# A decoder layer on one core: FFN weight scales spread by a DRAM round trip instead of matmuls with diagonals, and w_q loaded behind the seventh expert

## The chip, the core and the metric

The kernel runs on one core of one Trainium2 chip. The metric is device time in microseconds (us) from start to end of one execution; lower is better. The engines are named as in the profile: PE (TensorE, matmuls; PEld is its weight load), DVE (VectorE), ACT (ScalarE), POOL (GpSimd) and SP (SyncE, which here issues DMAs only).

## The reference, cut to what matters

One decoder layer in three parts, each added to the residual and followed by a layer norm: a Mamba block with a mixture of experts, a cross-attention, and a feed-forward with 8-bit weights and activations.

```python
# x: (4, 256, 256); 1024 tokens of 256.  Every token goes to 2 of 8 experts.
x = layernorm(x + moe(mamba(x)))
# cross-attention: 16 heads of 128, 64 keys for each batch entry
q = rmsnorm((x @ Wq).reshape(B, Sq, H, D), gq)
k = rmsnorm((ctx @ Wk).reshape(B, Skv, H, D), gk)
x = layernorm(x + (softmax(q k^T / sqrt(D)) (ctx @ Wv)) @ Wo)
# feed-forward, every linear with fp8 weights and one scale for each output row
def qlinear(qx, scale_x, scale, W, idx, out_idx=None):
    Wr = W[:, idx]
    w_scale = max(abs(Wr), axis=1, keepdims=True) / 448
    qw = fp8(Wr / w_scale)
    y = (qx * scale_x) @ (qw * w_scale).T * scale
    return y if out_idx is None else y[:, out_idx]
t = silu(qlinear(qx, sx, sc, w_gate, up_idx, down_idx)) * qlinear(qx, sx, sc, w_up, up_idx, down_idx)
x = layernorm(x + qlinear(quantised t, ..., w_down, down_idx))
```

The change concerns `w_scale`: 704 scales of `w_gate`, 704 of `w_up`, 256 of `w_down`. They are worked out with one weight row on each partition, so that a chunk of 128 scales is a column (`w_scale[:, m, chunk]`, m = 0, 1, 2). They are used as factors along the free dimension of token tiles, so each partition needs all of them in a row (`scale_rows[m]`).

## The kernel before

All tensors that live for a part of the kernel are views of one buffer, `arena`, by address in KB; the names `arena` and `ps` (the eight PSUM banks) are therefore all that the profile shows of most operands. Every engine has a program written out by hand, in the order in which it runs; engines wait for each other on counting semaphores (`pe.wait_ge(s["x_normed"], 4)`). No scheduler moves anything.

The part of the program that matters runs from the experts to the start of the attention:

- **Experts.** For each of the 8 experts PE runs a tail of 64 rows and then a loop of full tiles of 128 rows (matmuls L2177 up, L2185 down). POOL gathers the rows of each tile from DRAM (L466) and scatters the results to `moe_out` in DRAM (L499). The weights of expert e are loaded by SP (L303) into `w_moe[e % 2]`, two buffers at 163 KB (even experts) and at 16.5 KB (odd ones), when the expert two before is done. Beside the experts DVE quantises the FFN weights in pieces (`quantise`, L1275; its tables are `QUANT_AHEAD` and `QUANT_BEHIND`), and in that leaves `w_scale`. `gate_tail` (L1439) is DVE's part of an expert's tail, for which PE waits (L2122).
- **After the experts.** PE transposes the last keys (L2101) and multiplies keys by `w_qT` (L2200: 16 pairs of matmuls; ACT takes each from PSUM, L891). Meanwhile SP waits until all results are stored, loads them back in four parts (`y_got`, L347) and then loads `w_q` (L348, 2 MB, into 16.5 KB). DVE adds the parts to `x` (`add_results`, L1510), takes the variances and normalises the first four tiles (L1508), which raises `x_normed` to 4; then it does the same for the other four.
- **Scales.** DVE multiplies `w_scale[:, 1]` by `down_one` (L1493) and makes three sets of diagonal matrices from the columns (L1494, helper L1069). PE multiplies them by a matrix of ones (`spread_scales`, helper L1927), in three places: before the transposes of `x` (L2214), behind them (L2323) and behind the first scores (L2327). ACT copies each result to `scale_rows` (`take_scales`, L895). The buffer of `scale_rows` is the one that the experts' rows come into, hence PE's wait for the last gather (L2203).
- **Attention and FFN.** PE then runs the list at L2322 ff.: transposes of `x` (`transpose_x1`, L2220; DVE copies one bank, L1525, ACT the other, L903), scores of a token tile (L2239), queries (L2250), transposed probabilities (L2262), values (L2271), and between them the FFN of earlier tiles (L2286 gate and up). DVE's `take_gate` (L1595) and `take_up` (L1599) read `scale_rows[0]` and `[1]`, `add_result` (L1631) `scale_rows[2]`.

## Time and profile before

| | |
|---|---|
| three timed runs, us | 634.47, 634.90, 635.46 (median 634.9) |
| profiled execution, first to last instruction, us | 633.6 |
| PE busy | 586.3 us (93%) |
| DVE busy | 468.6 us (74%) |
| ACT busy | 386.8 us (61%) |
| POOL busy | 299.3 us (47%) |
| chain that ended last | PE 70%, ACT 12%, DVE 9%, issue 5%, DMA 2% |
| mean granted TensorE clock | 0.988 of full speed |

The times are of whole executions, the profile is of one more execution; its span leaves out what lies before the first and behind the last instruction, and the median is 1.3 us above it. The busy shares are means over a program of very different stages: the scan of the Mamba block (to about 245 us) is set by DVE and ACT, the experts (to about 442 us) by PE with short waits for DVE, the attention with the FFN by PE up to about 576 us, and the last 57 us by chains that go back and forth between DVE, PE and ACT. The chain of waits follows the end of the program back, from each instruction to the one that released it.

### The profile page before, as it was taken

To read this page: it belongs to the slowest core of one execution; us is meant where nothing else is said; L and a number is where in the kernel's file an instruction comes from. 1 tells how busy PE (TensorE), PEld (TensorE's weight loads), DVE (VectorE), ACT (ScalarE), POOL (GpSimd) and SP (SyncE) were. 2 spreads that over 40 slices of the span, in tenths; PEclk is the share of its full clock that TensorE was granted. 3 is DMA by queue.
4 is the path that set the end of the run, shared out by engine and by line. 5 is a ranking of instruction groups with operands and counts; after the bars stand their busy time and mean duration, and the time that the engine had idled before them with its cause. 6 is when DMAs were issued, how large, how long until landed. Compare 5 with 4: busy or idle time off the path is not lost.

```text
span 633.6 us, 10935 instructions
## 1 busy us (share of the span) xinstructions
PE 586.3 (93%) x3641; PEld 443.9 (70%) x3641; DVE 468.6 (74%) x793; ACT 386.8 (61%) x880; POOL 299.3 (47%) x239
## 2 busy tenths in 40 slices
PE   4999689998999999999999999999999999998874
PEld 2653579887998888597779779778855555665542
DVE  6989999999999976534553543563655789998885
ACT  4689899999999956522232231321746665687543
POOL 6032599999999991123232334344112232225101
PEclk9999899999999999999999999999999999999898
DMA  8001552121121008334441441411700000000002
GB/s 286 2 1 38 168 221 61 51 61 57 51 64 55 34 17 322 109 141 171 171 150 55 171 170 34 171 43 28 274 1 1 1 2 0 1 1 1 2 0 67
DMA packets 18261, 51.50 MB, mean 81 GB/s; under 512 B 3842, under 2 KB 9603, under 8 KB 16548
## 3 DMA queue, kind: packets, MB, share of 16 engines
q1 hardware_dynamic: 15172, 41.43, 19.0%
q0 software_dynamic: 2752, 7.34, 4.0%
q10 hardware_dynamic: 288, 2.10, 0.9%
q8 instruction: 27, 0.44, 0.3%
q14 instruction: 22, 0.18, 0.1%
HBM read 46.21 MB, written 4.66 MB: 80 GB/s over the span
## 4 chain that ended last, share of the span: by engine, by line
PE 70%; ACT 12%; DVE 9%; issue 5%; DMA 2%; POOL 0%; POOLq 0%; DVEq 0%; ACTq 0%
PE ps L2177 11%; PE ps L2250 8%; ACT arena L672 7%; PE ps L2185 6%; PE ps L2239 4%; PE ps L2271 4%; ACT arena L687 3%; PE ps L1960 3%; PE ps L1945 3%; PE ps L1994 2%; PE ps L2200 2%; PE ps L1786 2%; PE ps L2117 2%; PE ps L1795 2%; PE ps L1947 2%
## 5 line engine op out<-in xcount | busy, mean ns | idle before, releaser
L449 POOL TENSOR_TENSOR arena<-arena 128x1024 f32<-128x1024 f32 x63 | 147.3, 2391 | 3.4 <-DVE arena L1305 3.1
L1305 DVE TENSOR_TENSOR_SCAN arena<-arena,ps 128x1024 f32<-128x1024 f32 x64 | 143.4, 2279 | 4.0 <-ACT arena L672 0.9
L672 ACT ACTIVATE arena<-arena,a_neg 128x510 f32<-128x510 f32 x128 | 84.6, 709 | 1.9 <-DVE arena L1305 1.7
L2177 PEld LDWEIGHTS ps<-arena 128*128 128x128 f32 x660 | 75.4, 192 | 3.4 <-issue 3.1
L2177 PE MATMUL ps<-arena 128*128 128x128 f32 x660 | 77.0, 276 | 0.0
L1945 PE MATMUL ps<-ident,arena 128*128 128x128 f32 x384 | 64.7, 278 | 9.9 <-ACT arena L683 8.5
L1960 PE MATMUL ps<-ident,arena 128*128 128x128 f32 x512 | 67.3, 273 | 2.5 <-DVE arena L1314 1.8
L882 ACT ACTIVATE arena<-ps 128x256 f32<-128x256 f32 x45 | 17.3, 384 | 82.5 <-PE ps L2177 82.5
L687 ACT ACTIVATE arena<-arena,b_tok 128x512 f32<-128x512 f32 x96 | 64.8, 709 | 0.0
L1960 PEld LDWEIGHTS ps<-ident,arena 128*128 128x128 f32 x512 | 57.8, 141 | 4.1 <-DVE arena L1314 1.3
L2250 PE MATMUL ps<-arena 128*128 128x512 f32 x128 | 58.2, 595 | 0.0
L1945 PEld LDWEIGHTS ps<-ident,arena 128*128 128x128 f32 x384 | 45.7, 143 | 14.6 <-ACT arena L683 12.8
L1947 PE MATMUL ps<-arena 128*128 128x128 f32 x256 | 49.9, 277 | 0.0
L528 POOL TENSOR_TENSOR q_rs<-q_ms,neg_half 128x16 f32<-128x16 f32 x8 | 23.6, 2948 | 51.5 <-DVE q_ms L1555 51.5
L914 ACT ACTIVATE arena<-ps 128x128 f32<-128x128 f32 x128 | 33.5, 279 | 17.9 <-PE ps L2250 17.8
L2185 PE MATMUL ps<-arena 128*128 128x256 f32 x180 | 41.3, 379 | 0.0
L1482 DVE TENSOR_TENSOR arena<-arena,ps 128x256 f32<-128x256 f32 x30 | 12.6, 421 | 37.9 <-ACT arena L882 37.4
L499 POOL DMA_INDIRECT moe_out<-arena,result_now x23 | 23.8, 1035 | 34.8 <-DVE arena L1490 21.4
L2250 PEld LDWEIGHTS ps<-arena 128*128 128x128 f32 x128 | 23.5, 190 | 23.7 <-issue 20.8
L1947 PEld LDWEIGHTS ps<-arena 128*128 128x128 f32 x256 | 39.1, 193 | 0.0
L2185 PEld LDWEIGHTS ps<-arena 128*128 128x128 f32 x180 | 33.0, 190 | 3.9
L466 POOL DMA_INDIRECT arena<-hn_rows,row_now x23 | 25.4, 1105 | 18.2 <-POOL row_now L484 18.2
(313 smaller groups left out, 1143.6 us busy)
## 6 DMA issues: line engine op xcount, KB each, us to landing
arena<-in_w_moe SPq DMA_DIRECT2D x8, 2176.0 KB, 9.0
arena<-c_dram SPq DMA_DIRECT2D x32, 256.0 KB, 3.2
arena<-in_w_o ACTq DMA_DIRECT2D x1, 2048.0 KB, 13.1
arena<-in_w_qT SPq DMA_DIRECT2D x1, 2048.0 KB, 11.5
arena<-moe_out SPq DMA_DIRECT2D x8, 256.0 KB, 4.7
arena<-in_w_q SPq DMA_DIRECT2D x1, 2048.0 KB, 10.2
x<-in_x SPq DMA_DIRECT2D x2, 512.0 KB, 4.5
arena<-in_w_in SPq DMA_DIRECT2D x2, 512.0 KB, 5.6
```

What stands on the lines that cost most here:

```text
L449: pool.tensor_tensor(in_chunks(hC[unit % 3]), in_chunks(h[unit % 3]), c_bc[:, m % C_BUFS, :].unsqueeze(1).to_broadcast([P, 2, HALF]), ALU. ...
L466: pool.indirect_dma_start(row_in, None, hn_rows[:, :], bass.IndirectOffsetOnAxis(index, 0)).then_inc(s["ld_rows"], 16)
L672: ins = nc.scalar.activation(dA_b[:, unit % 2, 2 * k:2 * k + 2, 1:], dt_b[:, c, 2 * half:2 * half + 2, 1:], ACT.Exp, scale=a_neg[:, c, n:n ...
L687: nc.scalar.activation(sdtx[m % 2][:, i, :], dtxT[:, HALF_TILES * half + i, :], ACT.Identity, scale=b_tok[:, HALF_TILES * half + i, n:n + ...
L914: ins = nc.scalar.activation(q_junk[:, g % 2, hd * DH:(hd + 1) * DH], ps[:, g % 2, hd * DH:(hd + 1) * DH], ACT.Square, scale=float(DH) ** ...
L1305: nc.vector.tensor_tensor_scan(h[unit % 3], dA[:, k, :], ps[:, 2 * k:2 * k + 2, :].rearrange("p a b -> p (a b)"), 0.0, ALU.mult, ALU.add). ...
L1945: ins = nc.tensor.transpose(dst, sdtx[m % 2][:, i, c * P:(c + 1) * P], ident[:, :])
L1947: ins = nc.tensor.matmul(dst, dtxT[:, HALF_TILES * half + i, c * P:(c + 1) * P], b_diag[m % 2], start=True, stop=True)
L1960: return nc.tensor.matmul(ps[:, bank, c * P:(c + 1) * P], part, ident[:, :], start=first, stop=last, is_transpose=ADD_TRANSPOSED, skip_gro ...
L2177: ins = nc.tensor.matmul(ps[:, bank, c * P:(c + 1) * P], w13[:, k, chunk * P:(chunk + 1) * P], xT[:, k, :], start=(k == 0), stop=(k == KD ...
L2185: ins = nc.tensor.matmul(ps[:, 6, 0:D], hid[:, c, :], w2[:, c, :], start=(c == 0), stop=(c == FCH - 1))
L2250: ins = nc.tensor.matmul(ps[:, g % 2, :], tokens(t, k), w_q[:, k, g * HALF:(g + 1) * HALF], start=(k == 0), stop=(k == KD - 1))
```

## The change

The scales no longer pass through DVE, PE and ACT. DVE multiplies `w_scale[:, 1]` by `down_one` in the turn of expert 3 and signals it. SP, once it has issued the weights of expert 5, writes all 14 columns of `w_scale` to DRAM in the transposed order (1792 single values of 4 bytes), and later reads them back into every partition in one broadcast (`all_scales`, 7 KB for each partition, at the old address of `scale_rows`). It does so when PE has finished the ninth of the 16 pairs at L2200; PE's wait for the last row gather moves from behind these pairs to before the ninth. DVE waits for the read before the first `take_gate`. DVE's diagonals, PE's spread matmuls and ACT's copies are gone, with the waits around them.

`w_q` gets the even experts' buffer (163 KB) and is loaded when expert 6, the last to use it, is done; PE waits for it on `ld_o`. `y_got`, `shift` and `soft`, which were there, move to the odd experts' buffer (16.5 KB).

```diff
+SCALES = 2 * FCH + KD
-        y_got = [view(163, [TILES, D]), view(171, [TILES, D])]
+        y_got = [view(16.5, [TILES, D]), view(24.5, [TILES, D])]
-        w_qT, w_q = view(0, [HEADS, D]), view(16.5, [KD, HEADS * DH])
+        w_qT, w_q = view(0, [HEADS, D]), view(163, [KD, HEADS * DH])
-        shift, soft, pT = view(163, [2, HEADS, KV]), view(171, [2, HEADS, KV]), view(0, [2, PAIRS, P])
+        shift, soft, pT = view(16.5, [2, HEADS, KV]), view(24.5, [2, HEADS, KV]), view(0, [2, PAIRS, P])
-        diag = [view(87.5, [FCH, P]), view(66.5, [FCH, P]), view(69.5, [KD, P])]
+        all_scales = view(56.5, [SCALES * P])
+        scale_dram = nc.dram_tensor("scale_dram", (1, SCALES * P), F32).ap()
+        SCALES_READY_AT, SCALES_STORED_AT, ROWS_LANDED_AT = 3, 4, 8
...
                 load_weights(e + 1)
+                if e == SCALES_STORED_AT:
+                    sp.wait_ge(s["scales_ready"], 1)
+                    sp.dma_start(scale_dram.rearrange("o (k p) -> p (o k)", p=P), w_scale[:, :, :].rearrange("p m c -> p (m c)")[:, 0:SCALES],
+                                 allow_slow_non_contiguous=True).then_inc(s["ld_idx"], 16)
+            done = sp.value_load(bounds[0:1, E - 1:E], min_val=1, max_val=OUT_TILES)
+            sp.wait_ge(s["y_ready"], done + 1)
+            load(w_q, inp["w_q"], "ld_o")
             total = sp.value_load(bounds[0:1, E:E + 1], min_val=E, max_val=OUT_TILES)
             sp.wait_ge(s["y_stored"], total * 16)
...
-            load(w_q, inp["w_q"], "ld_kq")
+            sp.wait_ge(s["kv_psum"], QK_AT + ROWS_LANDED_AT + 1)
+            sp.wait_ge(s["ld_idx"], 96)
+            load(all_scales, scale_dram.partition_broadcast(P), "ld_idx")
...
-            take_scales(0)
             take_result_half(0)
-            take_scales(1)
-            take_scales(2)
             mean_squares(0, 0, 1, 2, 3)
...
+                if e == SCALES_READY_AT:
+                    nc.vector.tensor_tensor(w_scale[:, 1, :], w_scale[:, 1, :], down_one[:, :], ALU.mult).then_inc(s["scales_ready"], 1)
                 gate_tail(e, last)
...
-            link(nc.vector.tensor_tensor(w_scale[:, 1, :], w_scale[:, 1, :], down_one[:, :], ALU.mult))
-            for m, chunks in enumerate((FCH, FCH, KD)):
-                diagonals(diag[m], w_scale[:, m, 0:chunks], chunks).then_inc(s["counted"], 1)
...
                 dve.wait_ge(s["ff_psum"], 2 * t + 1)
+                if t == 0:
+                    dve.wait_ge(s["ld_idx"], 112)
...
                 bank = kv_bank()
+                if n == ROWS_LANDED_AT:
+                    pe.wait_ge(s["ld_rows"], last * 16 + 32)
...
-            pe.wait_ge(s["ld_rows"], last * 16 + 32)
...
-            spread_scales(0)
...
             transpose_x1(0)
-            spread_scales(1)
             pe.wait_ge(s["kv_out"], kv[0])
             pe.wait_ge(s["x1T_done"], 2)
             scores_of(0)
-            spread_scales(2)
-            pe.wait_ge(s["ld_kq"], 48)
+            pe.wait_ge(s["ld_o"], 32)
             queries_of(0, 0, 1, 2, 3)
-            pe.wait_ge(s["spread_done"], 5)
             transpose_x1(1)
```

How the instructions stand on PE behind the last pair at L2200, before (a program's list of each engine's instructions with the semaphores that they wait for; L1927 are the spread matmuls, L2220 the transposes of `x`, L2239 the first scores, L2250 the first queries):

```order
L1927 MATMUL ps<-arena,ones 128x512 [waits kv_out,counted,ld_rows]
L1927 MATMUL ps<-arena,ones 128x256
L2220 MATMUL ps<-ident,x 128x128 [waits x_normed]
L2220 MATMUL ps<-ident,x 128x128 x7
L1927 MATMUL ps<-arena,ones 128x512 [waits kv_out,counted]
L1927 MATMUL ps<-arena,ones 128x256
L2239 MATMUL ps<-arena 128x512 [waits x1T_done,kv_out]
L2239 MATMUL ps<-arena 128x512 x3
L1927 MATMUL ps<-arena,ones 128x256 [waits spread_done,counted]
L2250 MATMUL ps<-arena 128x512 [waits ld_kq]
L2250 MATMUL ps<-arena 128x512 x3
```

The five spread matmuls stand in three places among transposes, scores and queries. On the same engine and at the same place in the changed program (where L2201 are the transposes, L2220 the scores and L2231 the queries):

```order
L2201 MATMUL ps<-ident,x 128x128 [waits x_normed]
L2201 MATMUL ps<-ident,x 128x128 x7
L2220 MATMUL ps<-arena 128x512 [waits x1T_done,kv_out]
L2220 MATMUL ps<-arena 128x512 x3
L2231 MATMUL ps<-arena 128x512 [waits ld_o]
L2231 MATMUL ps<-arena 128x512 x3
```

The five are gone; transposes, scores and queries follow each other in the same order. SP's list in the changed program from the weights of expert 5 on (L306 are expert weights, L347 the write of the scales, L280 all other loads; the ISA and REGISTER rows fetch the tile counts that its waits use):

```order
L306 DMA arena<-in_w_moe 128x4352 [waits y_ready]
L347 DMA scale_dram<-w_scale 128x14x1 [waits scales_ready]
...
L306 DMA arena<-in_w_moe 128x4352 [waits y_ready]
...
L280 DMA arena<-in_w_q 128x4096 [waits y_ready]
L352 TENSOR_LOAD bounds
L352 ISA x2
L353 REGISTER_ALU
L280 DMA arena<-moe_out 128x2x256 [waits y_stored]
L280 DMA arena<-moe_out 128x2x256 x7
L280 DMA arena<-scale_dram 128x1792 [waits ld_idx,kv_psum]
```

Before, nothing stood between the expert weights and the loads of `moe_out`, and `w_q` was behind these as SP's last load; now `w_q` is before them, the write of the scales is between the weights of experts 5 and 6, and their read is the last load.

## Rows read from the trace of the kernel before

**Rows 1.** Chain of waits, 442 to 504 us: start us, length us, what.
```profile
444.64 13.81 PE ps L2200 x64
458.46 1.29 PE ps L1927 x4
...
460.62 1.29 PE ps L1927 x4
461.91 3.43 PE ps L2239 x8
465.35 0.43 PE ps L1927 x2
...
502.93 1.19 PE ps L2286 x8
```
**Rows 2.** Timeline of DVE, 443 to 474 us: start, length, instruction, [idle before it, releaser].
```profile
443.60 2.16 DVE L1069 TENSOR_TENSOR arena<-ident,w_scale 128x768 f32<-128x768 f32 x3
449.62 1.67 DVE L1518 SCALAR_TENSOR_TENSOR x<-arena,prob,x 128x256 f32<-128x256 f32 x4 [3.86 <-DMA arena<-moe_out]
...
452.37 1.67 DVE L1518 SCALAR_TENSOR_TENSOR x<-arena,prob,x 128x256 f32<-128x256 f32 x4 [0.41 <-DMA arena<-moe_out]
...
457.48 1.36 DVE L1508 TENSOR_SCALAR x<-x,mv,rs 128x256 f32<-128x256 f32 x4
...
473.86 0.17 DVE L1555 TENSOR_SCALAR q_ms<-q_ms 128x16 f32<-128x16 f32 x1 [5.20 <-ACT arena L914]
```
**Rows 3.** Timeline of PE and ACT around the first scores.
```profile
459.58 1.04 PE L2220 MATMUL ps<-ident,x 128*128 128x128 f32 x8
...
460.66 0.60 ACT L903 ACTIVATE arena<-ps 128x512 f32<-128x512 f32 x1
...
461.75 3.60 PE L2239 MATMUL ps<-arena 128*128 128x512 f32 x8
...
465.62 7.03 PE L2250 MATMUL ps<-arena 128*128 128x512 f32 x16
```
**Rows 4.** DMA issues: what, by which queue, count, KB each, median us to landing.
```profile
arena<-in_w_q SPq DMA_DIRECT2D x1, 2048.0 KB, 10.2
```
**Rows 5.** DMA queues, whole program: packets, MB, share of 16 engines' span.
```profile
q1 hardware_dynamic: 15172, 41.43, 19.0%
```
**Rows 6.** DMA queues, 18 to 22 us, where L300 reads single values.
```profile
q1 hardware_dynamic: 1009, 0.00, 12.8%
```
**Rows 7.** Timeline of DVE and PE at the tail of expert 3.
```profile
328.09 0.19 DVE L1284 RECIPROCAL w_inv<-w_scale 128x6 f32<-128x6 f32 x1
...
328.66 0.11 DVE L1442 MEMSET arena<- 64x64 f32 x1 [0.38 <-PE ps L2117]
...
329.41 0.22 DVE L1446 TENSOR_TENSOR arena<-arena,ps 64x64 f32<-64x64 f32 x1
...
329.69 0.55 PE L2125 MATMUL ps<-ident,arena 128*128 128x128 f32 x3
```
**Rows 8.** Row gathers (L466): all, and in the chain of waits the longest.
```profile
DMA to landing us min/median/max: 2.7/3.1/7.0
...
268.45 6.96 DMA arena<-hn_rows,row_now
```
**Rows 9.** Timelines: DVE in expert 5, POOL in expert 7; chain in expert 7.
```profile
381.40 0.42 DVE L1452 COPY arena<-ps 64x256 f32<-64x256 f32 x1 [3.21 <-POOLq L491]
...
424.33 0.99 POOL L466 DMA_INDIRECT arena<-hn_rows,row_now  x1 [0.79 <-POOL row_now L484]
...
431.37 0.22 PE ps L2087 x2
```
**Rows 10.** Windows near the end: us, busy (x) of PE, PEld, DVE, ACT, POOL; clock; DMA.
```profile
582.00:588.00 6.00, 3.24 (x18) 2.50 (x18) 5.86 (x10) 3.17 (x13) 2.91 (x1) 0.72 0.02 4
588.00:594.00 6.00, 6.00 (x28) 4.56 (x27) 4.71 (x6) 4.46 (x6) 1.68 (x1) 0.71 0.00 1
...
612.00:618.00 6.00, 2.96 (x18) 1.16 (x16) 5.62 (x10) 2.65 (x5) 0.00 (x0) 1.00 0.00 0
```

More of the change, by code:

```diff
@@ L231, in build @@
             s_shifted s_exp s_soft pT_psum pT_done attn_psum attn_taken eps4 rstd_x2 ld_idx ld_late gathered_w0
-            gathered_w1 iota_done counted spread_psum spread_done quantised wT_psum wT_done x_scaled x_size_ready x_quant
+            gathered_w1 iota_done scales_ready spread_psum spread_done quantised wT_psum wT_done x_scaled x_size_ready x_quant
             xT8_psum xT8_done ff_psum ff_read ff_gate ff_in t_scaled t_in_ready t_size_ready prod_done t_done t_psum
@@ L893, in _ @@
                 step += 1
-            def take_scales(m):
-                act.wait_ge(s["spread_psum"], 3 + m)
-                bank = (4, 6, 4)[m]
-                width = (FCH, FCH, KD)[m] * P
-                nc.scalar.activation(scale_rows[m], ps[:, bank:bank + 2, :].rearrange("p a b -> p (a b)")[:, 0:width], ACT.Identity).then_inc(s["spread_done"], 1)
             def take_result_half(half):
@@ L1066, in _ @@
             dve.wait_ge(s["iota_done"], 1)
-            def diagonals(dst, col, chunks):
-                return nc.vector.tensor_tensor(dst, ident[:, :].unsqueeze(1).to_broadcast([P, chunks, P]),
-                                               col.unsqueeze(2).to_broadcast([P, chunks, P]), ALU.mult)
             def compare_up():
@@ L1637, in _ @@
             add_epsilon(0)
-            dve.wait_ge(s["spread_done"], 5)
             take_result_half(1)
@@ L1922, in _ @@
             transpose_inputs(1, 1)
-            def spread_diagonals(diagonals, chunks, bank):
-                for at in range(0, chunks, 4):
-                    n = min(4, chunks - at)
-                    ins = nc.tensor.matmul(ps[:, bank + at // 4, 0:n * P], ones[:, :], diagonals[:, at:at + n, :].rearrange("p a b -> p (a b)"), start=True, stop=True)
-                ins.then_inc(s["spread_psum"], 1)
-            SPREAD_BANKS = (4, 6, 4)
             def inputs_of(unit):
@@ L2202, in _ @@
                 ins.then_inc(s["kv_psum"], 1)
-            pe.wait_ge(s["ld_rows"], last * 16 + 32)
-            def spread_scales(m):
-                pe.wait_ge(s["counted"], 1 + m)
-                if m == 2:
-                    pe.wait_ge(s["spread_done"], 3)
-                else:
-                    pe.wait_ge(s["kv_out"], kv[0] - 4 + 2 * m)
-                spread_diagonals(diag[m], (FCH, FCH, KD)[m], SPREAD_BANKS[m])
-            spread_scales(0)
             def transpose_x1(half):
```

## Prediction, written before the changed kernel ran

> **What bounds the kernel now.** I read the chain of waits first, since the busy shares are means over stages with different limits. From 442 to 576 us it is PE almost without a break, and the three places where the change takes work away stand in it as pieces of their own: 1.29, 1.29 and 0.43 us of L1927 among the pairs of L2200, the scores and the queries [rows 1]. So PE sets the time where the spread matmuls stand, and what they take, 3.01 us in sum, is the most that their removal by itself can return. The chain does not say what is late next. For that I read the timelines of DVE, ACT and PE just there. The first four tiles of `x` are normalised at 457.48 + 1.36 = 458.84 us [rows 2], while PE ends L2200 at 458.46 [rows 1]. PE was never seen waiting for DVE because the first spread filled the gap; without it, DVE is 0.4 us late.
>
> **The change part by part.**
>
> *Before the transposes.* DVE's L1508 ends at 458.84 [rows 2]. PE starts about 0.06 us after the DVE instruction that it waits for: L1446 ends at 329.63, L2125 starts at 329.69 [rows 7]. So the transposes start at 458.90; before, it was 459.58 [rows 3], a gain of 0.68.
>
> *Between transposes and scores.* The scores need both copied banks. The eight transposes take 1.04 us, to 459.94. ACT's L903 started 0.04 us after their end (459.58 + 1.04 = 460.62; it started at 460.66) and took 0.60 [rows 3]. So the copy ends at 459.94 + 0.04 + 0.60 = 460.58, and the scores start 0.06 later, at 460.64. Before, it was 461.75 [rows 3], since the second spread stood there; it covered the copy, so its 1.29 us bring only another 0.43. The gain so far is 1.11. ACT is free for L903: the copies of the scales that stood around it are gone.
>
> *Between scores and queries.* Scores to queries took 465.62 - 461.75 = 3.87 us [rows 3], 0.43 of it the third spread [rows 1]. Without it the queries start at 460.64 + 3.44 = 464.08, which is 1.54 us sooner. That is the sum: 3.01 us of PE work go, 1.54 arrive, and the rest becomes two gaps on PE, some 0.4 us for `x_normed` and some 0.7 us for the copy.
>
> *From there to the end.* Every later instruction of PE, ACT, DVE and POOL hangs on the queries and scores, or on work that was early. DVE comes to the first scores only some 0.7 us sooner (its own chain of adds is unchanged), but it then waited 5.20 us for the queries' squares [rows 2], so it takes up the whole 1.54. The lists are otherwise the same, so I carry the 1.54 to the end undiminished.
>
> *DVE's diagonals.* They took 2.16 us from 443.60, and then DVE sat idle for 3.86 us until the first part of the results had come from DRAM [rows 2]. Their removal lengthens that wait: nothing.
>
> *DVE's multiplication in expert 3.* It is one instruction on 128x6 like the reciprocal before it, 0.19 us [rows 7]. It stands between this reciprocal, which ends at 328.28, and `gate_tail`, whose L1442 sat idle for 0.38 us waiting for PE [rows 7]. PE's wait is the cover: nothing. Without the cover it would be 0.19, since PE starts L2125 right behind L1446.
>
> *The write of the scales.* 1792 values of 4 bytes, from SP, beside expert 4's gathers. The trace has no such write. The nearest row is L300's reads of single values: 1009 packets took 12.8% of 16 engines in 4 us, 8.2 us of engine time, 8.1 ns each [rows 6]. At that price 1792 take 14.5 us of engine time, 0.9 us on 16 engines. The upper end is the mean packet of the queue, which carries 2.7 KB: 19.0% of 16 x 633.6 us over 15172 packets is 127 ns [rows 5], 14.2 us on 16 engines. I take 0.9, the row with the same size of packet. What hides it: SP has nothing to issue until the next weights, and the row gathers that share the engines usually land in 3.1 us [rows 8], while PE comes for a row some 7 us after its gather (424.33 to 431.37, in a loop that is the same for all full tiles) [rows 9]. The longest gather took 7.0 us [rows 8], so even that would be in time, barely. Cost nothing; at the upper end perhaps 0.5 us for one late gather.
>
> The Trainium skill's page "DMA: Bandwidth & Descriptors" (Rules for kernel authors) says that a strided last dimension becomes one descriptor for each element, and its Specifications that transfers under 512 B are read, modified and written back. The trace agrees with the first (1009 packets for some 960 values); no row shows the second. If it doubles the price, the write takes an estimated 1.8 us, which the same slack hides.
>
> *w_q in expert 7.* It took 10.2 us to land [rows 4] and did not hold PE: the queries followed the scores. Now it is loaded some 40 us sooner, so it cannot hold them either. It runs beside expert 7's gathers, as expert weights do in experts 2 to 6. There DVE waits up to 3.21 us for a result to be stored (L1452) [rows 9], but PE's chain shows no wait for it. I take nothing. The upper end is a late gather: one of 7.0 us, issued at 424.33, would land at 431.33, just before PE's 431.37. A gather of 8.5 us would cost 1.5.
>
> *The read of the scales.* It is issued after nine of 16 pairs, at about 444.64 + 9 x 0.86 = 452.4 [rows 1], behind the result loads in its queue. 0.9 MB should need less than `w_q`'s 10.2 us for 2 MB [rows 4], so it lands by 463; the first gate matmuls start at 502.93 [rows 1]: 40 us of cover. DVE's new wait is never felt. PE's earlier wait for the last gather comes some 7 us after that gather was due: nothing.
>
> **The rivals.**
>
> (a) *The result loads land sooner.* DVE waited 0.41 us for the second part [rows 2], with `w_q` queued right behind these loads. If `w_q` slowed them, its move brings up to 0.41 more: 1.95 in all, 632.95. Against: the loads of one queue start in order. PE's end of L2200 forbids more.
>
> (b) *Less arrives.* If the copies or the DVE adds start later than worked out, for instance behind the read of the scales, only the third spread and a little more are gained, about 0.5: 634.4.
>
> (c) *A stalled gather.* `w_q` or the write of the scales holds one gather for 8.5 us instead of at most 7.0 [rows 8]; PE stands 1.5 us and the gain is used up: 634.9. Speaking for it: the longest gather, 6.96 us, was in the chain [rows 8].
>
> (d) *Slower: the clock falls in the new gaps.* PE now idles some 1.1 us between 458.4 and 460.7 where it had no idle time. In 582 to 594 us, with PE busy 3.24 us of the first six, the granted clock was 0.72 and 0.71 (stretches at 1.2 instead of 2.4 GHz) [rows 10]. That is 0.28 x 6 + 0.29 x 6 = 3.4 us of PE work lost. The same fall here, where PE is the bound, ends at 634.9 - 1.5 + 3.4 = 636.8; it decides from a loss of 1.5. Against: in 612 to 618 PE was busy only 2.96 us of six and the clock stayed at 1.00 [rows 10], and my gaps are short.
>
> (e) *The late fall goes.* Everything behind 464 us shifts; if the fall at 582 does not come, another 3.4 go: 630.0. Against: the gap on PE before it is made by DVE and stays, and three runs lie within 1.0 us.
>
> **How the numbers follow.** The profiled execution spans 633.6 us, which becomes 632.1; the median of the timed runs is 634.9, 1.3 above the span, and I take the 1.54 from it: 633.4. Chances: this forecast 0.58, (a) 0.13, (b) 0.12, (c) 0.06, (d) 0.06, (e) 0.05. The range 632.2 to 635.2 holds the forecast, (a), (b) and (c) with the runs' scatter of half a us, and leaves (d) and (e) out. About 0.2% (1.3 us) is what a measurement of this kernel can tell from no change; that is 633.6, close to my forecast, so I count 0.40 of its 0.58 as faster and 0.18 as the same. Faster: 0.40 + (a) 0.12 + (e) 0.05 = 0.57. Same: 0.18 + (a) 0.01 + (b) 0.12 + (c) 0.04 = 0.35. Slower: (d) 0.06 + (c) 0.02 = 0.08.
>
> **What would show it.** In the chain of the changed kernel L1927 is absent, and between the pairs and the transposes a short piece of DVE (L1508's successor) or "issue" stands, then one of ACT before the scores. The pairs end when they did, the transposes start at about 458.9 and the queries at about 464.1. SP shows `w_q` issued near 420 and the scales' read near 452.5, with no DVE wait for it before the gate. I am wrong if PE waits for a gather in expert 4 or 7, if the clock is under 1.00 between 458 and 475, or if the last 60 us differ in length by more than 0.5 us.

## The result: slower by 0.75%, lost in expert 4

The changed kernel takes 640.16 us (median of six runs, 638.73 to 642.60), the kernel before 635.18 (six runs, 634.47 to 637.43). The ratio is 1.0075, with a 95% interval of 1.0057 to 1.0093. The profiled executions span 638.4 and 633.6 us.

To see where the 4.8 us lie, I cut both spans at four instructions that both kernels have: POOL's stores of the last tile of experts 3, 4, 6 and 7. First the kernel before, timeline of POOL (start us, length us, instruction, idle before it and its releaser):

```profile
350.35 0.99 POOL L499 DMA_INDIRECT moe_out<-arena,result_now  x1 [1.44 <-DVE arena L1490]
...
373.94 1.19 POOL L499 DMA_INDIRECT moe_out<-arena,result_now  x1 [1.44 <-DVE arena L1490]
...
420.59 1.20 POOL L499 DMA_INDIRECT moe_out<-arena,result_now  x1 [1.33 <-DVE arena L1490]
...
443.18 1.20 POOL L499 DMA_INDIRECT moe_out<-arena,result_now  x1 [1.45 <-DVE arena L1490]
```

The same four in the changed kernel, where the line is L511, with the gather (L478) behind the first of them:

```profile
351.29 0.99 POOL L511 DMA_INDIRECT moe_out<-arena,result_now  x1 [1.44 <-DVE arena L1491]
355.02 1.00 POOL L478 DMA_INDIRECT arena<-hn_rows,row_now  x1 [0.79 <-POOL row_now L496]
...
381.49 1.18 POOL L511 DMA_INDIRECT moe_out<-arena,result_now  x1 [1.44 <-DVE arena L1491]
...
428.13 1.20 POOL L511 DMA_INDIRECT moe_out<-arena,result_now  x1 [1.25 <-DVE arena L1491]
...
451.12 1.20 POOL L511 DMA_INDIRECT moe_out<-arena,result_now  x1 [1.45 <-DVE arena L1491]
```

With the start of the queries (465.78 before, 472.50 after, in the chains of waits) the span falls into six stages:

| stage | before, us | after, us | difference |
|---|---|---|---|
| start to the last store of expert 3 | 350.35 | 351.29 | +0.94 |
| expert 4 | 23.59 | 30.20 | **+6.61** |
| experts 5 and 6 | 46.65 | 46.64 | 0.0 |
| expert 7 | 22.59 | 22.99 | +0.40 |
| last store to the queries | 22.60 | 21.38 | -1.22 |
| queries to the end | 167.82 | 165.90 | -1.92 |

Expert 4 is where the scales are written. The first stage has nothing of the change but DVE's short multiplication; over all the kernels below it ends between 349.7 and 352.2 us, so its +0.94 is scatter.

**Expert 4.** The chain of waits of the changed kernel (start, length, what) shows a store of results that took 12.06 us to land. In DVE's list the copy of the tail's result (L1451) waits for that store to free its buffer, and the hidden product of the next tile (L1483) stands behind it; PE waits for the product.

```profile
351.29 12.06 DMA moe_out<-arena,result_now
...
363.41 0.43 DVE arena L1451
...
364.79 0.43 DVE arena L1483
...
365.26 2.93 PE ps L2168 x12
...
437.70 1.60 PE ps L2168 x12
```

PE's timeline shows the standstill, 3.42 us:

```profile
365.26 2.93 PE L2168 MATMUL ps<-arena 128*128 128x128 f32 x12 [3.42 <-DVE arena L1483]
...
368.41 4.07 PE L2176 MATMUL ps<-arena 128*128 128x256 f32 x12
```

Then PE ran slowly: the last two rows of the chain are the same twelve matmuls in experts 4 and 7, 2.93 and 1.60 us. The twelve of L2176 behind them took 4.07 us, where the next tile's take 2.76. Standstill and slow matmuls make some 6.1 of the 6.6 us. The windows (us, busy time of PE, PEld, DVE, ACT and POOL, granted clock, DMA share, GB/s) show the clock at 0.50, its lower level of 1.2 GHz, behind the standstill, and next to no DMA packet that begins between 360 and 364 us (the DMA share counts a packet where it begins):

```profile
358.00:360.00 2.00, 2.00 (x19) 2.00 (x18) 0.07 (x1) 0.45 (x1) 0.00 (x0) 1.00 1.07 85
360.00:362.00 2.00, 1.84 (x17) 1.65 (x15) 0.00 (x0) 0.50 (x2) 0.00 (x0) 1.00 0.00 0
362.00:364.00 2.00, 0.00 (x0) 0.00 (x0) 0.55 (x2) 0.26 (x1) 0.18 (x1) 1.00 0.04 2
...
366.00:368.00 2.00, 2.00 (x12) 2.00 (x11) 0.00 (x0) 0.00 (x0) 1.72 (x2) 0.50 0.14 33
```

POOL's queue (q0 of the DMA queues: packets, MB, share of 16 engines) moved the following from 351 to 360 us:

```profile
q0 software_dynamic: 96, 0.26, 15.8%
```

That is 0.26 MB, one store and one gather of a tile of 0.13 MB each; from 360 to 362 us the queue moved a single packet of no size that shows. The packed trace has it packet by packet: 61 of the 64 packets of 4 KB that carry the two had ended by 360.04 us, and the last three, which took 1.33 to 4.28 us each, ended at 362.68, 364.01 and 364.13. Yet the store landed at 363.35, and the gather, issued at 355.02, is the one that took 11.0 us (rows 8 showed at most 7.0 [rows 8]):

```profile
DMA to landing us min/median/max: 2.7/3.1/11.0
```

The write of the scales had been queued from 350.87 us, behind the weights of expert 5, and all but a dozen of its packets had gone by 360.05.

A DMA raises its semaphore in 16 steps and has landed with the last; the packed trace has the time of each step. Of the store's steps 15 came between 357.91 and 359.19 us and the last at 363.34. The write's came between 363.76 and 366.14, and the gather's between 363.96 and 366.03. Taken in order, 15 of the gather's 16 follow one of the write's by 0.14 to 0.21 us. So the gather, most of whose data had moved by 360, was told as landed step by step with the write.

**Behind the experts** the profile reads as forecast in kind. Chain of waits, changed kernel, to be held against [rows 1]:

```profile
451.12 2.89 DMA moe_out<-arena,result_now
...
455.47 4.93 DMA arena<-moe_out
460.43 1.67 DVE x L1516 x4
...
465.62 1.29 DVE x L1506 x4
466.95 1.11 PE ps L2201 x8
468.08 0.61 ACT arena L909
468.83 3.67 PE ps L2220 x8
472.50 6.87 PE ps L2231 x16
```

The spread matmuls are gone, and the end of the pairs of matmuls no longer sets the transposes: it is now the landing of the results, through DVE's adds (L1516) and normalisation (L1506). PE's timeline has the two new gaps, 0.56 us for `x` and 0.78 for ACT's copy:

```profile
466.95 1.09 PE L2201 MATMUL ps<-ident,x 128*128 128x128 f32 x8 [0.56 <-DVE x L1506]
468.83 3.67 PE L2220 MATMUL ps<-arena 128*128 128x512 f32 x8 [0.78 <-ACT arena L909]
```

**The end.** The two windows in which the clock was 0.72 and 0.71 before [rows 10] are now:

```profile
582.00:588.00 6.00, 6.00 (x23) 3.07 (x21) 4.73 (x14) 4.37 (x18) 2.11 (x2) 1.00 0.00 0
588.00:594.00 6.00, 3.09 (x22) 1.85 (x20) 5.79 (x12) 4.17 (x18) 2.91 (x1) 1.00 0.00 1
```

The last stage has two lengths in the fourteen profiled kernels of this study, 165.8 to 165.9 us in eight and 167.1 to 167.8 in six. It is long in the two that keep the spread matmuls (the kernel before and the write alone) and in four of the other twelve. That alone cannot rule out a link to the change. But the kernel with the write behind the loads, one of the eight, has a mean granted clock of 0.988 over its twelve timed runs, the same as the kernel before over the 27 beside them.

### The profile page after: what moved, and what is told of

Same layout as the page of the kernel before. It is cut to its first block, busy times and chain, and to the rows that moved or that the text cites. A ratio compares the mean times of both kernels' runs of the same rounds, so it can differ in the third digit from the quotient of the medians.

```text
span 638.4 us, 10912 instructions
## 1 busy us (share of the span) xinstructions
PE 585.3 (92%) x3631; PEld 443.4 (69%) x3631; DVE 465.5 (73%) x790; ACT 384.6 (60%) x877; POOL 299.4 (47%) x239
## 4 chain that ended last, share of the span: by engine, by line
PE 61%; ACT 13%; DVE 11%; DMA 8%; issue 5%; POOL 1%; SPq 0%; DVEq 0%; POOLq 0%; ACTq 0%
PE ps L2168 10%; PE ps L2231 8%; ACT arena L684 7%; PE ps L2176 6%; DMA moe_out<-arena,result_now 5%; PE ps L2220 4%; ACT arena L699 3%; PE ps L2252 3%; PE ps L1951 3%; PE ps L1936 3%; PE ps L1985 2%; PE ps L1785 2%; PE ps L1794 2%; PE ps L1938 2%; DVE arena L1304 2%
## 5 line engine op out<-in xcount | busy, mean ns | idle before, releaser
L2168 PE MATMUL ps<-arena 128*128 128x128 f32 x660 | 79.1, 280 | 3.8 <-DVE arena L1483 3.7
L2168 PEld LDWEIGHTS ps<-arena 128*128 128x128 f32 x660 | 76.9, 195 | 7.8 <-DVE arena L1483 4.4
L2231 PE MATMUL ps<-arena 128*128 128x512 f32 x128 | 58.2, 595 | 0.0
L1938 PE MATMUL ps<-arena 128*128 128x128 f32 x256 | 50.3, 279 | 0.0
L2176 PE MATMUL ps<-arena 128*128 128x256 f32 x180 | 42.7, 389 | 0.0
L2231 PEld LDWEIGHTS ps<-arena 128*128 128x128 f32 x128 | 23.6, 191 | 24.1 <-issue 21.2
L511 POOL DMA_INDIRECT moe_out<-arena,result_now x23 | 23.8, 1034 | 34.5 <-DVE arena L1491 22.2
L1938 PEld LDWEIGHTS ps<-arena 128*128 128x128 f32 x256 | 39.4, 195 | 0.0
L2176 PEld LDWEIGHTS ps<-arena 128*128 128x128 f32 x180 | 34.1, 197 | 4.2
L1483 DVE TENSOR_TENSOR arena<-arena,ps 128x256 f32<-128x256 f32 x30 | 12.6, 421 | 33.4 <-ACT arena L894 31.4
L478 POOL DMA_INDIRECT arena<-hn_rows,row_now x23 | 25.4, 1104 | 18.2 <-POOL row_now L496 18.2
```

Source lines behind the costliest of these rows:

```text
L1938: ins = nc.tensor.matmul(dst, dtxT[:, HALF_TILES * half + i, c * P:(c + 1) * P], b_diag[m % 2], start=True, stop=True)
L2168: ins = nc.tensor.matmul(ps[:, bank, c * P:(c + 1) * P], w13[:, k, chunk * P:(chunk + 1) * P], xT[:, k, :], start=(k == 0), stop=(k == KD ...
L2176: ins = nc.tensor.matmul(ps[:, 6, 0:D], hid[:, c, :], w2[:, c, :], start=(c == 0), stop=(c == FCH - 1))
L2231: ins = nc.tensor.matmul(ps[:, g % 2, :], tokens(t, k), w_q[:, k, g * HALF:(g + 1) * HALF], start=(k == 0), stop=(k == KD - 1))
```

## The experiments

My theory was that the 1792 single values are the whole loss: while they are under way, row transfers of the experts land late. The rivals were `w_q` in expert 7, a place that merely happened to be bad, and the new code behind the experts. Each kernel is the changed one with the edit shown, unless said otherwise. The stage table behind the experiments holds the stages of all profiled runs.

**The write alone, on the kernel before.** DVE's multiplication moves to expert 3 and SP writes the scales in expert 4; the matmuls with diagonals stay.

```
+                if e == SCALES_STORED_AT:
+                    sp.wait_ge(s["counted"], 1)
+                    sp.dma_start(scale_dram.rearrange("o (k p) -> p (o k)", p=P), w_scale..., allow_slow_non_contiguous=True)
```

> The kernel before with one thing added: DVE multiplies w_scale[:, 1] in the turn of expert 3, and SP writes the 1792 scales to DRAM behind the weights of expert 5, as in the changed kernel; nothing reads them, and diagonals, spread matmuls and w_q stay as they were. Theory 1 (the write holds up the store of expert 3's last result tile; DVE waits in order for the one result row buffer, PE for DVE, and the clock falls in that gap): the store lands in about 12 us instead of 7.6, PE stands about 3.4 us in expert 4, the clock is at half for some 7 us behind it, and the time is about 6.5 us over before (3 to 7, as late falls of the clock come and go). Theory 2 (w_q beside expert 7 costs the time): no change against before.

Measured: 641.62 us against 635.93, ratio 1.0091 (1.0061 to 1.0121). Here not the store but the gather was held, and PE waited for it directly:

```profile
354.49 12.02 DMA arena<-hn_rows,row_now
...
366.55 0.44 PE ps L2095 x2
366.99 4.24 PE ps L2193 x12
```

Expert 4 takes 29.52 us, 5.9 more than before. The clock fell here too: twelve matmuls of 2.59 us (their length in the tile before) took 4.24. The write by itself costs as much as the whole change lost: 5.7 us here, 5.0 there.

**The write later in the same loop**, once the tail of expert 4 has been stored:

```
+                if e == SCALES_STORED_AT + 1:
+                    before = sp.value_load(bounds[0:1, e - 1:e], min_val=1, max_val=OUT_TILES)
+                    sp.wait_ge(s["scales_ready"], 1)
+                    sp.wait_ge(s["y_stored"], before * 16 + 16)
+                    sp.dma_start(scale_dram..., w_scale..., allow_slow_non_contiguous=True)
```

> The changed kernel with the write of the scales moved by some 12 us: SP waits until the tail of expert 4 has been stored and then writes, in the stretch in which no weights move, 10 us before the weights of expert 6. Theory 1: the store of expert 3's last tile lands in about 7.6 us as before, PE does not stand in expert 4 and the clock stays at 1.00 there; of the changed kernel's 6.6 us lost in expert 4 nearly all come back, so it is 5 to 7 us faster than the changed kernel and 0.5 to 2 us faster than before (the 1.2 us gained behind the experts less 0.4 us lost in expert 7). Theory 2: it stays at the changed kernel's time, about 5 us over before. If the write is bad for any store that it meets, the next store (full tile, 4 us later) lands late and some of it stays.

Measured: 642.27 us, ratio 1.0117 (1.0087 to 1.0147): a miss. The write, issued at 361.71 and no longer behind the weights, held the next gather instead:

```profile
363.24 10.58 DMA arena<-hn_rows,row_now
```

So the place was not a particularly bad one: at both places the write met a row transfer. But the hold looked different. The write's 1808 packets had gone by 363.8 us, and then the rows themselves moved slowly. In POOL's queue, from 362 to 374 us:

```profile
q0 software_dynamic: 96, 0.26, 24.3%
```

That is 46.7 us of packet time for this gather and the store behind it. Single packets of 4 KB took up to 4.03 us, where in the kernel before none at the like place took over 0.37. The write's steps came up to 372.50 us, the gather's up to 373.82.

**`w_q` behind the result loads**, the write unchanged:

```
-            done = sp.value_load(bounds[0:1, E - 1:E], min_val=1, max_val=OUT_TILES)
-            sp.wait_ge(s["y_ready"], done + 1)
-            load(w_q, inp["w_q"], "ld_o")
...
+            load(w_q, inp["w_q"], "ld_o")
             sp.wait_ge(s["kv_psum"], QK_AT + ROWS_LANDED_AT + 1)
```

> The changed kernel with w_q loaded behind the result loads again (still into 163 KB); the write of the scales stays where the change put it. Theory 1: expert 4 still loses 6 to 7 us; only the 0.4 us in expert 7 come back, perhaps less if the result loads get slower with w_q behind them; the time stays 4 to 6 us over before. Theory 2: it returns to before or below it.

Measured: 639.07 us, ratio 1.0055 (1.0032 to 1.0078). Expert 7 is back at 22.59 us; expert 4 still takes 27.37. Its store took 10.70 us and its gather 11.56:

```profile
354.55 11.56 DMA arena<-hn_rows,row_now
```

PE stood twice, for 2.05 and 1.12 us, and in this execution the clock stayed at 1.00 there. That splits the 6.6 us of the changed kernel: PE's standstill is 3.2 to 4.4 us in each of these runs, and where it came in one piece (3.42 us in the changed kernel, 3.90 with the write alone, 4.36 with the write later) slow matmuls follow; in two pieces they did not.

**The write in natural order**, one run of 56 bytes for each partition. The transposition is left out, so the scales come back in another order:

```
-sp.dma_start(scale_dram.rearrange("o (k p) -> p (o k)", p=P), ...
+sp.dma_start(scale_dram.rearrange("o (p k) -> p (o k)", p=P), ...
```

> The changed kernel with the scales written to DRAM in the order in which they lie: 128 runs of 56 bytes instead of 1792 single values, at the same place in the program and with as many bytes. The transposition is left out, so the scales that come back are in the wrong order; all times are those of the same work. Theory 1 in the form that the many single values are the cost (their packets fill the DMA engines and their completion holds back the store's): the store of expert 3's last tile lands in about 7.6 to 8.5 us, PE hardly stands in expert 4, and the time is 5 to 7 us under the changed kernel. A rival form, that any write to DRAM behind the weights holds the store: the store still lands in 11 to 12 us and the time stays.

Measured: 634.18 us against 635.93, ratio 0.9968 (0.9951 to 0.9985). No gather took over 6.0 us, no store over 8.5, and expert 4 takes 23.71. The same bytes at the same place hold nothing, so it is the way in which the single values are written. In expert 7 the chain still holds a store, with DVE's L1451 and PE behind it, which the kernels without `w_q` there do not show:

```profile
421.79 7.61 DMA moe_out<-arena,result_now
```

**Half the values.** Seven columns as single values, the other seven in natural order behind them:

```
+sp.dma_start(scale_dram[:, 0:half * P].rearrange("o (k p) -> p (o k)", p=P), ws[:, 0:half], allow_slow_non_contiguous=True)
+sp.dma_start(scale_dram[:, half * P:SCALES * P].rearrange("o (p k) -> p (o k)", p=P), ws[:, half:SCALES])
```

> The changed kernel, write of the scales at its place in expert 4, but only seven of its 14 columns (896 values) as single values; the other seven go in natural order as 128 runs of 28 bytes, so that half of the scales that are read back stand in another order. Theory A1 (the hold is made of the values' own time, in the engines and in the silence behind them): half the values hold half as long, the row transfer that meets them takes 3 + 4.3 = 7.3 us for a gather or 7.6 + 2.2 = 9.8 for a store; the slack of 7 us that PE has on a gather covers nearly all of it, PE stands under 1 us in expert 4 and the time is 633.5 to 635.5. Theory A2 (any such scattered write holds the queue for a fixed time, however many values): the gather again takes 11 to 12 us, PE stands 3 us or more, and the time is about 640 as for the changed kernel.

Measured: 638.63 us against 635.69, ratio 1.0047 (1.0029 to 1.0064). A gather was held nearly as long:

```profile
353.57 10.66 DMA arena<-hn_rows,row_now
```

PE stood for 2.54 us; expert 4 takes 26.48 us, 2.9 over before, with the clock at 1.00. Half the values do not halve the hold, so A1 falls. A2, a fixed hold with PE standing 3 us or more and some 640 us, is nearer and missed too. In this run the gather's data was clearly not what was late. POOL's queue from 351 to 360 us, with both the store and the gather in it:

```profile
q0 software_dynamic: 96, 0.26, 7.9%
```

The last of the 64 packets of 4 KB ended at 358.46 us, and the gather landed at 364.24, 5.8 us later (0.33 in the kernel before). The last step of the writes had come at 364.06.

**The write moved behind the result loads**, where no row transfer is under way, and then `w_q` too:

```
             for part in range(4):
                 ... # the eight result loads
+            load(w_q, inp["w_q"], "ld_o")      # second kernel only
+            sp.wait_ge(s["scales_ready"], 1)
+            sp.dma_start(scale_dram..., w_scale..., allow_slow_non_contiguous=True)
             sp.wait_ge(s["kv_psum"], QK_AT + ROWS_LANDED_AT + 1)
```

> The changed kernel, with the write of the scales issued behind the result loads, just ahead of the read of the scales, where no gather or store of an expert is under way; w_q stays in expert 7. Theory A (the 1792 single values hold whatever row transfer of the experts meets them, and that is the whole loss): expert 4 is as long as before (23.6 us between the store of its last tile and the one before, not 30.2), the three gains behind the experts stay (1.2 to 1.5 us), w_q costs the 0.35 us in expert 7 that the run with the write in natural order showed; the time is 1 to 2 us under before, 633 to 634, if the write doesn't hold the result loads, which are ahead of it in the same queue. The write's own landing can be read here from the wait of SP for it: 2.3 us or more of packets, and some 6 us from issue to landing or more if the silence of 3 us belongs to the write itself. Theory B (the write slows whatever is under way, the result loads too): the second part of the result comes later than 0.7 us behind the first in DVE's idle time, the transposes and scores move with it, and the time is that of before or above. Theory C (the loss is in the rest of the change, and only the early place of the write hid that): not under before.

> The changed kernel, with both the write of the scales and the load of w_q issued behind the result loads (w_q first, then the write, then the read of the scales). If the 0.35 us by which expert 7 is longer with w_q beside it are real, expert 7 takes 22.6 us here as before, and the time is some 0.35 us under that of the kernel with only the write moved, so about 633. If the queue delays the write behind w_q's 2 MB, the read of the scales starts some 10 us later, near 465, and lands by 475; the gate matmuls wait for nothing before 500, so no cost. If w_q beside the result loads slows them, the second part comes later and the gain is used up: then the two kernels are equal or this one is slower.

Measured: 635.07 us, ratio 0.9996 (0.9982 to 1.0010), and 634.80, ratio 0.9989 (0.9970 to 1.0009), against 635.69. Expert 4 is at 23.72 in both, expert 7 at 23.06 and 22.60. The loss is gone; that either is faster than before cannot be told from these runs, and A's 633 to 634 is missed by a us. By stages the first should have been 0.4 under before (+0.13, +0.47, -1.00), which is about what it was. The sign of Theory B, a second part of the results over 0.7 us late, came (0.93 us), but it decides nothing: the run with the write in natural order, with no such write near, has 0.91. SP's wait for the write shows why the hold is long:

```profile
SPq L358 <- DMA scale_dram<-w_scale: 10.8, 1, 10.8
```

**The write by itself.** Four kernels in which SP waits until the result loads have landed, issues the write with nothing beside it and waits for its landing: all 1792 values, 896, 128, or none as single values (what is left goes in natural order behind it).

```
+            for part in range(4):
+                sp.wait_ge(s[f"gathered{part}"], 32)
+            sp.dma_start(scale_dram[:, 0:cols * P].rearrange("o (k p) -> p (o k)", p=P), ws[:, 0:cols], allow_slow_non_contiguous=True)
+            sp.wait_ge(s["ld_idx"], 96)
```

> The changed kernel, the write of the scales issued alone: behind the result loads and only once these have landed, all 1792 values as single values, SP waiting for its landing before anything else is issued. It gives the price of this write by itself, in SP's wait and the DMA share. With nothing beside it, the packets should take some 1.4 to 2.5 us on the engines (the write behind the loads ended within 1.5 us of them) and the landing should come some 6 us after the last packet if the silence belongs to the write: 8 us or more from issue to landing. If the 10.8 us seen before were mostly queueing behind the result loads, 3 to 4 us.

> The same with 896 single values; the other seven columns follow in natural order in a second write once the first has landed (half of the scales then stand in another order). If packets and silence both go with the number of values: half the landing time of the 1792 (4 us where that is 8). If the silence is fixed, whatever the number: only the packets' 0.7 to 1.2 us less.

> The same with 128 single values, one for each partition, and the other thirteen columns in natural order behind it (52 bytes for each partition). If the silence goes with the number of values, it lands in some 2 to 3 us as any small transfer (the shortest row store lands in 2.3 us); if it is fixed, in 6 us or more.

> The same with no single values: the one write in natural order, 128 runs of 56 bytes (all scales then stand in another order). It should land in 2 to 3 us like a row store, which is why it held nothing in expert 4. If it too takes 6 us or more, the silence isn't what holds the gathers, and the number of packets would be.

Measured (one run each, so that the times tell little): 632.76, 632.40, 634.12 and 634.40 us, against 636.46 (nine runs of before, 635.10 to 637.54). SP's waits for the landing (us in total, times, longest), first of all 1792 values, then of 896:

```profile
SPq L362 <- DMA scale_dram<-w_scale: 10.1, 1, 10.1
```

```profile
SPq L361 <- DMA scale_dram<-w_scale: 7.8, 1, 7.8
```

Of 128 values, and in the same kernel of the 128 runs of 52 bytes that follow:

```profile
SPq L361 <- DMA scale_dram<-w_scale: 6.1, 1, 6.1
...
SPq L363 <- DMA scale_dram<-w_scale: 1.1, 1, 1.1
```

And of 128 runs of 56 bytes, with no single value:

```profile
SPq L360 <- DMA scale_dram<-w_scale: 1.5, 1, 1.5
```

As many packets, 128, land in 1.1 to 1.5 us when they carry 52 or 56 bytes and in 6.1 when they carry 4. The size is not all that differs: the 128 single values of a column are neighbours in DRAM, 512 bytes in all, where the runs of 56 bytes cover 7 KB. Single values written far apart were not tried, so that these runs do not tell the size from the place. From 128 to 1792 values it is another 4.0 us, 2.4 ns a value. The packets' own time is short all the while. For the 1792 values, the queue from 456.3 to 467 us, and the windows behind the issue at 456.38:

```profile
q1 hardware_dynamic: 1808, 0.01, 7.6%
```

```profile
457.00:459.00 2.00, 2.00 (x11) 1.75 (x10) 2.00 (x7) 1.47 (x3) 0.32 (x1) 1.00 0.41 4
459.00:466.00 7.00, 6.00 (x21) 3.02 (x20) 5.06 (x18) 1.35 (x3) 1.11 (x2) 1.00 0.00 0
```

7.6% of 16 engines in 10.7 us is 13.0 us of engine time, 7.2 ns a packet. It ended before 459; the landing, for which SP waits, came at 466.9. For some 8 us the write was out of the DMA engines and not done.

**The order that these runs point to**: `w_q` behind the result loads, then the write once all of that has landed, then the read.

```
+            load(w_q, inp["w_q"], "ld_o")
+            sp.wait_ge(s["scales_ready"], 1)
+            sp.wait_ge(s["ld_o"], 32)
+            for part in range(4):
+                sp.wait_ge(s[f"gathered{part}"], 32)
+            sp.dma_start(scale_dram..., w_scale..., allow_slow_non_contiguous=True)
+            sp.wait_ge(s["ld_idx"], 96)
```

> The changed kernel in the order that the runs point to: w_q behind the result loads, then, once these and w_q have landed, the write of the scales alone, and the read once the write has landed. Nothing that PE waits for is in flight in the 10 us of the write. By stages: expert 4 as in the runs with the write moved behind (23.7 us, 0.1 over before), expert 7 as before (22.6), from the last store to the queries 21.0 to 21.4 instead of 22.6. That is 1.1 to 1.5 us under before, 634.2 to 634.6 against 635.7; from the queries to the end 165.9 or 167.5 as in all runs. The write starts near 462, lands near 472, the read lands near 478, and the gate matmuls at 500 wait for nothing. If the scales come too late after all, DVE's first gate instruction waits for the load and the end moves by that much.

Measured: 634.24 us against 635.81, ratio 0.9971 (0.9954 to 0.9987): level with the write in natural order, and under the kernel before as well as the changed one. The stage behind the experts missed its 21.0 to 21.4: it took 21.97. DVE's timeline says why: the second part of the results came 1.24 us late.

```profile
455.04 1.67 DVE L1518 SCALAR_TENSOR_TENSOR x<-arena,prob,x 128x256 f32<-128x256 f32 x4 [1.24 <-DMA arena<-moe_out]
```

That idle time was 0.24 with the 1792 values written alone and 0.69 in the changed kernel, and the stage follows it: 21.04, 21.38 and 21.97 us. The profiled stages of this kernel give only 0.5 us in place of 1.6. Part of the rest is the end of the program: the mean granted clock of its twelve runs is 0.990, that of the kernel before beside it 0.988, and in the 27 runs of before that stood beside the moved write, those at 0.991 were 2.7 us shorter than those at 0.985. By that slope (an estimate) some 0.9 us of the 1.6 go with the clock. Whether the new order makes the late falls rarer or had luck is not settled.

| profiled kernel | expert 4 | expert 7 | last store to queries | queries to end |
|---|---|---|---|---|
| before | 23.59 | 22.59 | 22.60 | 167.82 |
| changed | 30.20 | 22.99 | 21.38 | 165.90 |
| write alone, on before | 29.52 | 22.59 | 22.60 | 167.58 |
| write later in the loop | 29.85 | 23.13 | 20.86 | 167.51 |
| `w_q` behind the loads | 27.37 | 22.59 | 21.02 | 165.86 |
| natural order | 23.71 | 22.94 | 21.68 | 165.89 |
| half the values | 26.48 | 22.92 | 21.37 | 167.12 |
| write behind the loads | 23.72 | 23.06 | 21.60 | 165.89 |
| the same, and `w_q` | 23.72 | 22.60 | 21.37 | 167.18 |
| by itself: 1792 / 896 | 23.71 / 23.72 | 23.05 / 23.12 | 21.04 / 21.33 | 165.85 / 165.87 |
| by itself: 128 / none | 23.72 / 23.72 | 22.95 / 22.95 | 21.36 / 21.26 | 165.86 / 167.55 |
| `w_q`, then the write | 23.72 | 22.59 | 21.97 | 165.8 |

Each row is one execution. In four kernels (the write later, `w_q` behind the loads, half the values, the write behind the loads) it is 1.7 to 2.8 us under the median of the timed runs, so that their other executions may well have lost more in these stages, or to the clock.

## Why the prediction was wrong

**The step that failed is the write of the scales, taken as "cost nothing".** Its engine time was right: 8.1 ns a packet was taken from the reads [rows 6], 7.2 were measured, and 0.9 us on 16 engines came out as 0.8. What failed is the sentence that this is the write's price, with the slack of 7 us as its cover. The write keeps the engines busy for under 2 us but is finished only ten us after its issue, and a row transfer that is under way meanwhile is held. Mostly it is told as landed only with the write, though its own data has moved; with the write later its packets were slow themselves. Gathers took 10.6 to 12.0 us, where the longest before was 7.0 [rows 8]. The slack that I named, 7 us, was near: PE came for the held gather 8.2 us after its issue with the write alone and with half the values, and 6.3 with the write later, which was 2.5 to 4.3 us too short. For a store beside the write, which is what stopped PE in the changed kernel, the prediction named no slack at all.

The upper end of the range, "0.5 us for one late gather" from 14.2 us of packets, was worked out from the wrong quantity as well: it took the time on the engines for the time to landing. None of the rows ahead held a write of small packets with its landing, and I took the nearest reads without saying that landing is another quantity.

The Trainium skill's page "DMA: Bandwidth & Descriptors" (Queues, rings and completion order) says, of the transfers that SP and ACT issue, that the semaphore increment is a strongly ordered write, which lands only after every earlier write of that DMA engine, across its queues. The changed kernel fits it, for a transfer of POOL's: the gather's steps, at 363.96 to 366.03 us, follow those of SP's write. I had not weighed this rule. The same page of the Trainium skill, in its section "Anatomy of one DMA — SWDGE (gpsimd) path", puts a fixed 2.0 us on a transfer that POOL issues, most of it the receipt from memory. POOL's shortest here are near that (2.3 us for a store, 2.7 for a gather), SP's writes of 52 and 56 bytes below it (1.1 and 1.5), the single values far above (6.1 to 10.1). The doubling below 512 B, weighed in the prediction, does not show in the engine time: 7.2 ns against 8.1 for reads.

That the landing of the write ends the hold is read from the steps of the two semaphores. The gather's last came behind the write's last in the four other kernels in which a gather was held: 366.51 behind 366.33 us with the write alone, 373.82 behind 372.50 with the write later, 366.11 behind 366.07 with `w_q` behind the loads, 364.24 behind 364.06 with half the values. What the runs do not settle is why the write takes so long to be acknowledged, whether it is the 4 bytes or their being neighbours in DRAM, and why row packets were slow themselves where the write was the only other transfer.

**Rival (c)** had the mechanism, a gather stalled by the write, at 8.5 us and a price of 1.5. Gathers took 10.6 to 12.0, a store was held besides, and it had no word for what follows a standstill of PE: the half clock, some 2.7 us in the changed kernel (2.93 for 1.60 us in the chain above, and 4.07 for 2.76 in the twelve matmuls behind). **Rival (d)** named the clock and put it into the wrong place: in the gaps of 0.56 and 0.78 us it stayed at 1.00, in expert 4 it fell after 3.42 us.

**Behind the experts the sum held in kind.** Predicted were a gain of 1.54, transposes 15.72 us behind the last store, scores 17.46, queries 20.90. Measured: 15.83, 17.71, 21.22 (PE's timeline), so a gain of 1.22. Between the steps nothing failed by over 0.15 us. What was missed is that the landing of the second result part now sets this stage: DVE's idle time before it was taken as fixed at 0.41 [rows 2] and is 0.20 to 1.24 from run to run, us for us on the path. Rival (a), loads that land sooner without `w_q` behind them, falls: 0.20 to 0.93 in the nine profiled kernels with `w_q` long gone, 0.25 to 1.24 in the five with it behind.

**`w_q` in expert 7** was taken as nothing, with a late gather as its upper end. It costs 0.33 to 0.54 us: 22.92 to 23.13 in the nine profiled kernels that load it there, 22.59 or 22.60 in the five that don't. The late transfer is a store, not a gather. I had seen DVE wait 3.21 us for a store [rows 9] and found PE's chain free of it; that chain was of expert 7 without a load beside it.

**DVE's diagonals, DVE's multiplication, the read of the scales** cost nothing, as forecast: no wait for the read stands before the gate, and stages without the write are as long as before but for expert 4. Even where the write holds nothing there, it takes 23.71 or 23.72 us in place of 23.59, which no run explains.

**Rival (e)**, the late fall of the clock not coming, happened in the profiled run and gave 1.92 us back, without a link to the change that the runs could show. That is luck: without it this run would have been some 6.7 us longer than the one before, not 4.8.

## What to carry to other kernels

A DMA's price is the time until it is told as done, its own and that of the transfers under way beside it, and not the time of its packets: before a write of single values is put beside row transfers that an engine waits for, measure its landing by itself. Where a transposed write can't be avoided, it belongs where nothing waits, here behind the result loads. When an engine off the path is freed, look what lands last next: its scatter becomes the kernel's.

## What the runs showed that I had not expected

- 128 writes of 4 bytes to neighbouring places in DRAM land in 6.1 us, 1792 in 10.1, though the packets of the 1792 have gone some 2 us after the issue; 128 writes of 56 bytes land in 1.5.
- While such a write is out, a gather of another queue was told as landed 5.8 us after its last packet, with half the values; with the write later, packets of 4 KB took up to 4.03 us.
- After a standstill of PE of 3.42, 3.90 and 4.36 us in one piece the granted clock fell to 0.50 for several us; after 2.54, and after 2.05 and 1.12 with work between, it stayed at 1.00.
